# Half of batch 0's first layer issued directly behind the mean of batch 1's x, in the embedding stage of a two-layer model

## The reference, cut to what matters

```python
def _ln(x, g, b):
    m = jnp.mean(x, axis=-1, keepdims=True)
    v = jnp.mean((x - m) ** 2, axis=-1, keepdims=True)
    return (x - m) * jax.lax.rsqrt(v + EPS) * g + b
h = _ln(x, pw_g[pathway_ids], pw_b[pathway_ids])
h = _ln(h, cp_g[compartment_ids], cp_b[compartment_ids])
t = _ln(x, tm_g[time_steps], tm_b[time_steps])
m = x + _mlp_ln(memory_state, ...)[:, None, :]      # n and r likewise
s = _ln(x, ms_g[scale_type], ms_b[scale_type])
cat = jnp.concatenate([w[0] * h, w[1] * t, w[2] * m, w[3] * n, w[4] * r, w[5] * s], axis=-1)
return _mlp_ln(cat, int_W1, int_b1, int_W2, int_b2, int_g, int_be)
```

## Time and profile before

| | |
|---|---|
| Median of 3 runs | 1571.45 us (1570.2 to 1573.3) |
| The profiled execution: its own time | 1569.42 us |
| Its span in the trace | 1567.6 us |
| Mean granted TensorE clock | 0.962 of full |
| Busy: PE, DVE, ACT, POOL | 92%, 68%, 54%, 30% of the span |
| Matmul instructions of the first layer (L1187) | 128, the first at 719.58 us, the last at 873 us |

### The profile page before, as it was taken

The page is one execution under the profiler, slowest core; times in us unless marked ns, Lnnn a source line. Parts: engine busy times, 40 slices in busy tenths (PEclk is TensorE's granted clock), DMA queues, the critical chain, the costliest instruction groups (busy, mean ns, idle before and its releaser), DMA issues.

```text
span 1567.6 us, 20191 instructions
## 1 busy us (share of the span) xinstructions
PE 1435.7 (92%) x7399; PEld 980.7 (63%) x7404; DVE 1068.8 (68%) x1218; ACT 854.0 (54%) x1509; POOL 477.9 (30%) x140
## 2 busy tenths in 40 slices
PE   5898799689998989979998889999989999999997
PEld 3576333389797979643444333333368888888886
DVE  6997395899989899774343567777463565555655
ACT  2433456699999998532333278787632533333332
POOL 0999120089898888200332220000000000000000
PEclk7899999799999999999999999999999999999999
DMA  7110010511413211411213032443000000000000
GB/s 271 26 62 1 1 54 2 197 47 55 158 58 122 81 55 54 152 21 20 61 41 91 21 101 58 130 136 95 1 1 0 1 14 1 0 14 1 14 1 14
DMA packets 36624, 87.61 MB, mean 56 GB/s; under 512 B 8350, under 2 KB 24948, under 8 KB 32948
## 3 DMA queue, kind: packets, MB, share of 16 engines
q1 hardware_dynamic: 36532, 86.39, 16.5%
HBM read 68.10 MB, written 18.21 MB: 55 GB/s over the span
## 4 chain that ended last, share of the span: by engine, by line
PE 71%; DVE 10%; ACT 9%; DVEq 5%; issue 3%; POOL 1%; DMA 0%; ACTq 0%; SPq 0%
PE ps L1452 12%; PE ps L1461 12%; PE ps L1018 5%; PE ps L1320 4%; PE ps L1393 4%; PE ps L1187 4%; PE ps L1003 3%; ACT arena L1756 3%; DVE arena L2057 3%; ACT arena L1744 3%; PE ps L1308 3%; DVEq L2056 2%; PE ps L1004 2%; PE ps L1213 2%; PE ps L896 2%
## 5 line engine op out<-in xcount | busy, mean ns | idle before, releaser
L2619 POOL TENSOR_TENSOR arena<-arena 128x2048 f32<-128x2048 f32 x63 | 287.9, 4585 | 140.8 <-DVE arena L2157 139.7
L2157 DVE TENSOR_TENSOR_SCAN arena<-arena,ps 128x1024 f32<-128x1024 f32 x128 | 284.6, 2272 | 28.3 <-issue 19.4
L1756 ACT ACTIVATE arena<-arena,mam 128x511 f32<-128x511 f32 x256 | 166.1, 714 | 22.5 <-DVE arena L2157 22.5
L1934 ACT ACTIVATE arena<-ps,rho 128x512 f32<-128x512 f32 x256 | 158.9, 688 | 34.0 <-PE ps L1393 32.6
L2391 DVE TENSOR_REDUCE mxs<-ps 128x1 f32<-128x512 f32 x224 | 141.1, 684 | 45.0 <-PE ps L1308 43.1
L1003 PE MATMUL ps<-early,arena 128*128 128x128 f32 x768 | 129.6, 277 | 15.4 <-DVE arena L2157 10.3
L1963 ACT ACTIVATE arena<-arena 128x256 f32<-128x256 f32 x192 | 85.5, 500 | 81.6 <-DVE arena L2562 50.3
L1452 PE MATMUL ps<-early,arena 128*128 128x256 f32 x512 | 127.1, 380 | 2.9 <-DVE mam L2558 1.8
L2599 POOL TENSOR_TENSOR arena<-arena 128x4096 f32<-128x4096 f32 x16 | 115.0, 7189 | 43.3 <-DVE arena L2076 43.3
L1744 ACT ACTIVATE arena<-arena,early 128x512 f32<-128x512 f32 x192 | 124.1, 712 | 3.9 <-DVE arena L2135 3.9
L1461 PE MATMUL ps<-arena 128*128 128x256 f32 x512 | 121.0, 379 | 1.2 <-issue 1.2
(11 more groups left out here) (349 smaller groups left out, 2471.1 us busy)
## 6 DMA issues: line engine op xcount, KB each, us to landing
arena<-bc_scratch SPq DMA_DIRECT2D x32, 512.0 KB, 3.7
arena<-in_ffn SPq DMA_DIRECT2D x8, 1024.0 KB, 4.9
batch_scratch<-arena SPq DMA_DIRECT2D x2, 3072.0 KB, 9.4
arena<-batch_scratch SPq DMA_DIRECT2D x6, 1024.0 KB, 6.8
arena<-q_scratch SPq DMA_DIRECT2D x96, 64.0 KB, 2.2
arena<-k_scratch SPq DMA_DIRECT2D x96, 64.0 KB, 2.2
arena<-in_dec_w SPq DMA_DIRECT2D x1, 3855.0 KB, 16.1
arena<-in_cond SPq DMA_DIRECT2D x1, 3739.5 KB, 11.5
```

Of the source, the lines that this page charges most:

```text
L1756: last = act.activation(decay[:, (2 * k + h) % 3, i, 1:S], dt[b % 2][:, m, 1:S], ACT.Exp, scale=a_neg[:, m * NS + n:m * NS + n + 1])
L1934: act.activation(pt[:, j % 4, i], ps[:, 3 + (hg + n) % 3, :], ACT.Exp, scale=rho[:, 0:1]).then_inc(s_pt, 1)
L2157: dve.tensor_tensor_scan(half, view(decay[:, (2 * k + h) % 3], [[1, 2 * S]]), view(ps[:, FEED + 2 * h, :], [[1, 2 * S]]), 0.0, ALU.mult, A ...
L2619: pool.tensor_tensor(state[:, k % SLOTS], state[:, k % SLOTS], view(c_rows[:, j % 2, k % G, :], [[0, M], [1, S]]), ALU.mult).then_inc(s_hc, 1)
```

## The change

TensorE's list alone is changed, and there for batch 0 alone. `first_layer(0, 0)` now stands directly behind the mean of batch 1's x, ahead of the variance of that norm and of `names(1)`. `first_layer(0, 1)` moves up to the place that `first_layer(0, 0)` had, so that nothing of the first layer is left between `places(1, 1, 1)` and the variance of `hh[1]`. No instruction is added or removed.

```diff
             pe.wait_ge(s_x2, B + 1)
             ln_mean(pe, norm, xT[:, :, tok(1)], B // 2 + 1)
-            ln_var(pe, norm, B // 2 + 1)
             pe.wait_ge(s_prep, 7)
             for b in range(B):
                 a = b + 1
+                if b == 0:
+                    first_layer(0, 0)
+                    ln_var(pe, norm, B // 2 + 1)
                 if a < B:
                     pe.wait_ge(s_kf, a)
                     names(a)
-                first_layer(b, 0)
+                first_layer(b, 0 if b else 1)
                 if a < B:
                     pe.wait_ge(s_h1, a + 1)
                     ln_mean(pe, norm, hh[a % 2], B // 2 + 2 * a)
                     places(a, 1, 1)
-                first_layer(b, 1)
+                if b:
+                    first_layer(b, 1)
                 if a < B:
                     ln_var(pe, norm, B // 2 + 2 * a)
```

## The result

The changed kernel takes 1563.63 us in the median of five runs (1561.92 to 1565.76), against 1571.45 for the kernel before in the same series (five runs, 1570.2 to 1573.3). A second series, in which both were run again, gave 0.9961 (0.9948 to 0.9975), 1564.03 against 1569.01 us. The profiled execution of the changed kernel took 1562.96 us, with a span of 1561.2; that is 6.4 us less than the span before.

What follows compares the result with a forecast made beforehand. TensorE was taken to bound the kernel (busy 92%, chain on it 71%). Gains of 2.39 and half of 2.01 us against 2.68 of new waits gave -0.7, from 1571.45 to 1570.7 us; range 1567.1 to 1574.1.

Steps and rivals of the forecast that it cites:

- (1): Between mean and variance of batch 1's x: TensorE's wait for the square goes, 2.39 us gained.
- (3): Ahead of the variance of `hh[1]`: a new wait of 1.58 us for its square, plus 0.25 for the restart.
- (4): Ahead of `second_layer(0)`: a new wait of 0.60 us for the SiLUs, plus 0.25 for a start from idle.
- The slack of `scaled`: VectorE's time between `scaled` and the `embed` behind it: shrinks from 1.37 to about 0.7 us and holds.
- The sum: From the mean's end at 708.49 to `second_layer(0)`: 27.59 us in the new order, 29.31 before.
- Step (2): Variance of batch 1's x: with the gap filled the clock stays full, 2.01 us gained; half, 1.0, taken for the runs.
- is passed on: Whatever is saved or lost before `second_layer(0)` starts at 737.80 reaches the end, since everything behind hangs on that start.
- rival (D): The shifted start moves a low clock stretch behind it away or brings another: 3 us either way, 1567.7 or 1573.7; chance 0.14.
- the one pair of rows that shows it: Sixteen q-product instructions: 7.15 us in batch 0 behind idle 1.11, 10.12 in batch 2 behind idle 2.83.
- rival (B): Around `hh[1]` and the SiLUs no new waits come, all 4.40 us are kept: 1567.1 us; chance 0.05.
- The base: The kernel before's median, 1571.45 us, 2.03 above its profiled execution, to which the -0.7 was applied.

Runs made afterwards that it cites:

- null_before: The kernel before, unchanged, timed again against itself: 1568.33 us, ratio 0.9996.
- before_plus_3_4: The kernel before with eight more matmul instructions (3.44 us) directly ahead of `second_layer(0)`: 1572.27 us, ratio 1.0023 to the kernel before.
- gap_filled: The kernel before with four unused matmul instructions (1.72 us) between the mean of batch 1's x and its variance: 1563.87 us, ratio 0.9975 to the kernel before.
- again_after: The changed kernel, unchanged, run again in a second series: 1564.03 us, ratio 0.9961 to the kernel before.
- after_plus_1_7: The changed kernel with four more matmul instructions (1.72 us) ahead of `second_layer(0)`: 1569.59 us, ratio 1.0001 to the kernel before.
- half_only: The changed kernel with `first_layer(0, 1)` back in its old place, only `first_layer(0, 0)` early: 1568.83 us, ratio 0.9999 to the kernel before.
- silu_first: The changed kernel with ScalarE's `first_silu(0)` ahead of the square of `hh[1]`, TensorE's order kept: 1570.88 us, ratio 0.999 to the kernel before.
- silu_and_second: The changed kernel with `first_silu(0)` ahead of the square of `hh[1]` and `second_layer(0)` ahead of its variance: 1563.95 us, ratio 0.9979 to the kernel before.
- before_plus_1_7: The kernel before with four more matmul instructions (1.72 us) directly ahead of `second_layer(0)`: 1566.76 us, ratio 0.9988 to the kernel before.
- second_plus_1_7: silu_and_second with four more matmul instructions (1.72 us) ahead of `second_layer(0)`: 1570.37 us, ratio 0.9996 to the kernel before.

## Why the prediction was wrong

**The local steps were right.** (1) The wait of 2.39 us is gone, the `embed` was in time. (3) and (4): waits of 1.59 and 0.59 us where 1.58 and 0.60 were worked out, with 1.31 us from the end of the square to the first SiLU and the table load between them. The Trainium skill's 2.66 us for a switch ("ScalarE: Activation LUTs", section "What ACT_TABLE_LOAD costs") would have given a second wait of some 1.95 us, and the trace doesn't bear it out. The slack of `scaled` was 0.71 us in the trace (the wait of VectorE for `scales` behind it); about 0.7 was forecast. The sum was 27.59 us and the trace shows 27.67.

**Step (2) was weighed too low.** I counted half of the clock's 2.0 us, since I held that the gap costs the clock in some executions alone. In all six profiles of kernels with this gap (before, null_before and the four with work added to it) the clock fell at it: the variance took 3.55 to 3.68 us in five of them and 2.49 in before_plus_3_4, where the names behind it took the rest of the low stretch. From the start of the variance to that of the first layer all six have 8.69 or 8.70 us. gap_filled, with 7.01 us there, shows that the gap is the cause. The term of the sum is thus close to 2.0 and the local gain 1.6 us (1.4 where the work before took its other way, again_after against before_plus_3_4 less its 3.44 us), not 0.7. It moved the forecast by 1 us.

**The step that failed** is the sentence that what is saved between 708.49 and 737.80 "is passed on", and with it rival (D). The 800 us behind the edit don't keep their length when they are shifted: 764 to 773 us for one and the same work. I had priced this rival at one low stretch (3 us), either way, with 0.14, from the one pair of rows that shows it; between the eighteen profiles it is worth up to 8.7 us, nearly three times that, and it isn't even-handed: none of them has a longer stretch than the profiled kernel before, so from that place a shift could only keep or shorten it. The pair of rows held more than I took: the same sixteen instructions in 7.15 and in 10.12 us told that the kernel before stood badly at that place. It didn't tell which moves would help; after_plus_1_7, half_only and silu_first moved and stayed at 770.9 to 772.2. The range's lower end came from rival (B), which stayed away, and not from (D) at its full size.

**The base was off as well.** The three runs of before that were known, 1570.2 to 1573.3, stand high; in the later series its medians were 1568.9 to 1570.0. Whether that was the draw or another chip is open. Of the 7.8 us some 2 are this, 1.6 us are the edit at its place, and the rest, about 4 us, is put down to the later work's better stand against the clock. (In the two profiles, 6.4 us apart, it is 1.6 at the place, 3.0 behind it, and 1.7 ahead of the edit, which the edit didn't make.) That last share is an estimate over executions and goes with the place of the edit, not with its idea: 0.86 us more of work ahead of it left the time nearly the same (ratio 0.9971 against 0.9961), 1.72 us took all of it away (1.0001).

**What was shown and what wasn't.** Shown are the local terms, the gap as the cause of one low stretch, and, in the profiles, that the later work's length goes with where it stands against the clock (eight kernels with a shift alone, four of them forecast). That the unprofiled runs do what the profiled ones do is an inference, from their groups and from the mean clock: over the 63 runs of before in the first two series the time falls as the clock rises (correlation -0.71; -0.73 over all 129 of the four series). Why the work before the edit comes out in two ways, and how often each, is open; so is a rule by which the costly places could be read from one trace. No kernel beat the changed one for certain: silu_and_second is 1.5 us shorter at the place and had 1563.95 against 1564.03 us in the same series, with ratios of 0.9979 and 0.9961.

## What to carry to other kernels

A local gain can be worked out from the trace to a tenth of a us and still not be what the whole execution shows: here idle times of 1.8 to 2.8 us cost TensorE its clock in some profiles and not in others, and moving later work by 1.7 us changed the whole by up to 0.4%. Test such a gain by the same shift made without the edit, forwards and backwards, before it is credited. And look at the kernel before for a place where equal instructions differ in length, since that tells whether it stands well or badly there; it doesn't tell which shift would help.

## What the runs showed of the hardware that was not expected

Added work didn't make the program slower (before_plus_1_7, -2.1 us in the median for +1.72 us of matmuls, ratio 0.9975 to 1.0002), and in the changed kernel, whose later work stood elsewhere against the clock, the same work made it slower by three times its size (after_plus_1_7, +5.6). A program on one core spreads by 9 us, 1562.2 to 1571.3 in 28 runs. Gaps of PE of 2.39 us (six profiles) and 2.72 us (one) were followed by a stretch at the lower clock in every profile that has them. The one of 2.83 us ahead of batch 2's q products was followed by it, or had it begin within the gap, in 13 of 18. A gap of 1.76 us ahead of L1207 was followed by it in second_plus_1_7 and not in silu_and_second. Gaps of 1.59 us ahead of the variance of `hh[1]` and of 0.69 us had none behind them.
